# Filter halves written straight into their slots, the other half by one copy each, and `vlo` at the head of its iteration

## The chip, the cores and the metric

One core of a Trainium2 chip runs the kernel. The metric is the device time of one execution in microseconds; lower is better. Five engines work side by side, each with its own queue: TensorE (PE; its weight loads are shown as PEld), VectorE (DVE), ScalarE (ACT), GpSimd (POOL) and SyncE (SP), which issues nearly all DMAs.

## The reference, cut to what matters

Four blocks, each adding to `x` (64 samples, 64 channels, 1024 columns, fp32) the output of four modulated convolutions:

```python
def _layer(x, style, w, b, mw, mb, typ):
    s = style @ mw.T + mb
    weight = SCALE * w * s[:, None, :, None]
    weight = weight * lax.rsqrt(jnp.sum(weight * weight, axis=(2, 3)) + EPS)[:, :, None, None]
    if typ == 'same':         out = vmap(_conv_same)(x, weight) + b[None, :, None]
    elif typ == 'upsample':   out = _blur(vmap(_conv_up)(x, ...) + b[None, :, None], 2.0 * blur_k, (1, 1))
    elif typ == 'downsample': out = vmap(_conv_down)(_blur(x, blur_k, (2, 2)), weight) + b[None, :, None]
    return out
# TYPES = ('same', 'upsample', 'same', 'downsample'), kernel size 3, SCALE = 1/24, blur 1 3 3 1
for k in range(4):
    x = x + layers_of_block_k(x, cond_512)
```

## The kernel before, in words

A sample lies in SBUF as 128 rows: 64 channels of the odd columns and 64 of the even ones, 512 columns each. Layer 1 is one convolution (`conv0`, six matmuls of 512 columns). Layers 2 to 4 with both blurs are merged, for each sample, into one filter of seven taps (`g`), and `convg` applies it in twelve matmuls of 512 columns. Every operand is split into a high part in fp32r and the rest (`xh`/`xl`, `zh`/`zl`, `gh`/`gl` and so on), and three products are added: high by high, low by high, high by low. ScalarE writes the high parts, VectorE the low ones.

The loop runs over n = 0 to 255 (sample and block). In its iteration n TensorE runs `conv0(n+1)`, then `convg(n)`. ScalarE runs `xhi(n+3)` and `zhi(n+1)`; VectorE `xlo(n+3)`, `xnew(n-1)` (adds the result to `X`) and `zlo(n+1)`. The filters are made once for a quad of four samples, on an order written out by hand:

- GpSimd scales the weights (`w3s`) and takes their low part (`w3lo`); ScalarE takes the high part (`w3hi`, L731).
- TensorE's `v_products` follow `convg` in iterations n = 1 mod 4. In the next iteration VectorE's `vfull` (L1001) evicts them to `vf`, and ScalarE's `vhi` (L737) writes `vh` in two instructions, L741 and L742.
- `vlo` (L1010) on VectorE has three instructions: `v4` (L1013), `vl` (L1015) and the last part of `vh` (L1017). It stands behind `zlo` in iterations n = 3 mod 4.
- TensorE's `k_products` stand at the head of iterations n = 0 mod 4 and need `vh` and `vl`. ScalarE evicts them to `kp` (`kev`, L752), in two parts around `zhi`; in the last block `xb` (L724), which adds a bias to `X`, follows at the end of each iteration.
- In the following iteration VectorE filters `kp` into `gf` (`fir_even`, `fir_odd`). One later ScalarE copies the two end taps to `gf` (L767) and rounds all of `gf` into `sh` (L769, in `ghi`), VectorE subtracts into `sl` (L1063, in `glo`).
- SP's `spread` (L332) copies from there to `gh` and `gl`. These hold three pairs of samples, each pair with two samples by eight slots of 64 columns. In the upper 64 rows the seven taps lie in slots 0 to 6, in the lower 64 rows in slots 1 to 7; the slot left over is zero. The filters of a quad's first pair are made in the upper rows of `gf`, those of the second pair in the lower rows, and either has to be in both halves: four DMAs for `gh` and four for `gl`, of 224 KB. Before a pair is overwritten SP waits for `convg` of the pair three back. `convg` of a quad's first sample waits for all four `gh` DMAs (`ghd`) before its first matmul, and for the four of `gl` (`gld`) before its ninth.

Table work for the next block (`setup`) and the edge columns (`edge`) are put behind the ordinary work in certain iterations, most of them n = 3 mod 4.

Of the kernel before, what the change touches and what calls it, by code (L numbers as in the profile page):

```python
# [7 lines left out]
F32 = mybir.dt.float32  # L8
# [46 lines left out]
NT = 7  # L55
BLUR_E, BLUR_O, BLUR_M, BLUR_SUM = 6.0, 15.0, 20.0, 32.0
KS = 10
EVEN, ODD, CORR, NONE = slice(1, 8, 2), slice(2, 8, 2), 0, 9
# [29 lines left out]
def build(nc, x, ends, pack, taps, w3in, small, sets, out):  # L88
    ctx = ExitStack()
    with ctx:  # L90
        def sb(name, shape, dt=F32):
            return ctx.enter_context(nc.sbuf_tensor(name, shape, dt))
# [44 lines left out]
        sh = sb("sh", [128, 2, NT, C], F32R)  # L137
        sl = sb("sl", [128, 2, NT, C], F32R)
# [95 lines left out]
        def by_tap(a):  # L234
            return a.rearrange("p i t c -> p t i c")

        def landed(q):

            return 16 * (2 + 4 * q)
# [62 lines left out]
        def _(sp):  # L302
# [29 lines left out]
            def spread(q):  # L332

                first, second = 2 * q, 2 * q + 1
                for name, ready, of, to in (("ghd", "gsh", sh, gh), ("gld", "gsl", sl, gl)):
                    sp.wait_ge(s[ready], q + 1)
                    for h, rows in ((first, slice(0, C)), (second, slice(C, 128))):
                        if q == 0 and h == first:
                            continue
                        if h >= 3:  # L340
                            sp.wait_ge(s["convg"], 2 * (h - 2))
                        src = of[rows, :, :, :].bitcast(F32)
                        sp.dma_start(to[0:C, h % 3, :, 0:NT, :].bitcast(F32), src).then_inc(s[name], 16)  # L343
                        sp.dma_start(to[C:128, h % 3, :, 1:NT + 1, :].bitcast(F32), src).then_inc(s[name], 16)  # L344
# [301 lines left out]
        def _(act):  # L646
# [115 lines left out]
            def ghi(q):  # L762

                act.wait_ge(s["fir"], q + 1)
                if q >= 1:
                    act.wait_ge(s["ghd"], landed(q - 1))
                act.activation(gf[:, 0:NT:NT - 1], kp[:, 1:8:6], ACT.Copy).then_inc(s["gfe"], 1)  # L767
                act.wait_ge(s["gfe"], q)
                act.activation(by_tap(sh[:, :, :, :]), gf[:, :, :, :], ACT.Copy).then_inc(s["gsh"], 1)  # L769
# [7 lines left out]
            def ghi_rest():  # L777

                act.wait_ge(s["fir"], 1)
                act.activation(by_tap(sh[C:128]), gf[C:128], ACT.Copy).then_inc(s["gsh"], 1)  # L780
# [60 lines left out]
            for n in range(2, NN):  # L841
                if n + 3 < NN:
                    xhi(n + 3)
# [13 lines left out]
                if v_at(n + 2) is not None:  # L857
                    w3hi(v_at(n + 2))
# [5 lines left out]
        def _(dve):  # L864
# [195 lines left out]
            def glo(q):  # L1060
                dve.wait_ge(s["gsh"], q + 1)
                dve.wait_ge(s["gld"], landed(q - 1))
                dve.tensor_tensor(by_tap(sl[:, :, :, :]), gf[:, :, :, :], by_tap(sh[:, :, :, :]).bitcast(F32), ALU.subtract).then_inc(s["gsl"], 1)  # L1063
# [7 lines left out]
            def glo_rest():  # L1071
                dve.wait_ge(s["gsh"], 1)
                dve.tensor_tensor(by_tap(sl[C:128]), gf[C:128], by_tap(sh[C:128]).bitcast(F32), ALU.subtract).then_inc(s["gsl"], 1)
# [106 lines left out]
            for n in range(2, NN):  # L1180
                due = g_at(n - 1)
                if due is None and n + 3 < NN:
                    xlo(n + 3)
                xnew(n - 1)
                if due is not None:
                    dve.wait_ge(s["kev"], due + 1)
                    dve.wait_ge(s["gsh"], due)
                    fir_even(whole, both)
# [12 lines left out]
                if v_at(n - 2) is not None and n - 2 not in V_LATE:  # L1201
                    vlo(v_at(n - 2))
# [310 lines left out]
```

## Time and profile before

| | us |
|---|---|
| median of 3 runs (1399.49 to 1403.38) | 1401.16 |
| the profiled execution | 1402.98 |
| its span, first to last instruction | 1401.2 |
| TensorE busy in the span | 1325.6 |
| VectorE busy | 1101.9 |
| ScalarE busy | 784.6 |
| GpSimd busy | 327.1 |

The profile is of one execution. Busy time is the union of an engine's instructions; the end of a matmul is modelled, so a weight load (PEld) shows a stall more fully than a matmul does. "Idle before" is the time in which an engine had nothing to run ahead of an instruction, with the instruction or DMA that ended it.

### The profile page before, as it was taken

The numbers are of one execution on the slowest core, as the hardware profiler recorded it, in microseconds if no ns is written. First come the engines' busy times: TensorE is split into PE (matmuls) and PEld (weight loads), VectorE is DVE, ScalarE is ACT, GpSimd is POOL, SyncE is SP. The second block draws the span as 40 slices with busy tenths as digits, with TensorE's granted clock in tenths as the row PEclk, the third lists the DMA queues.
The fourth block names the chain that finished last, engine by engine and source line by source line (L and its number), as shares of the span: only waits on it lengthen the run. The fifth ranks groups of instructions, "written<-read, shape, count | busy, mean of one in ns | idle before, by whom it ended". The sixth has DMA issues, their size and how long they took to land.

```text
span 1401.2 us, 20330 instructions
## 1 busy us (share of the span) xinstructions
PE 1325.6 (95%) x6565; PEld 1085.8 (77%) x6565; DVE 1101.9 (79%) x1792; ACT 784.6 (56%) x1465; POOL 327.1 (23%) x632
## 2 busy tenths in 40 slices
PE   7799999999999999999999999999999999999998
PEld 5587877787888788788788777788787777777776
DVE  6788788887787878888787788888787667778764
ACT  5556465655555555555555555555556466665663
POOL 2213211132213212114122211213212232222210
PEclk9899999999999999999999999999999989999999
DMA  8457867677876658877766867677865497687664
GB/s 298 117 122 195 210 177 193 167 186 204 219 188 174 168 162 219 211 183 199 168 190 185 218 175 197 148 187 205 225 184 155 106 182 192 175 220 189 180 165 114
DMA packets 148201, 257.51 MB, mean 184 GB/s; under 512 B 14784, under 2 KB 81344, under 8 KB 148096
## 3 DMA queue, kind: packets, MB, share of 16 engines
q1 hardware_dynamic: 147728, 255.93, 70.9%
q8 instruction: 54, 0.88, 0.3%
q14 instruction: 51, 0.42, 0.1%
q10 hardware_dynamic: 368, 0.28, 0.1%
HBM read 72.39 MB, written 67.24 MB: 100 GB/s over the span
## 4 chain that ended last, share of the span: by engine, by line
PE 41%; DVE 23%; ACT 10%; issue 9%; DMA 7%; SPq 7%; POOL 2%; ACTq 0%; DVEq 0%; POOLq 0%
PE ps L463 40%; DMA gl<-sl 7%; DVE zl L978 4%; SPq L343 4%; ACT kp L750 4%; SPq L344 3%; DVE gf L1029 3%; DVE xl L972 3%; DVE X L987 3%; ACT xh L709 2%; DVE vl L1015 2%; DVE v L1013 2%; DVE vf L1008 1%; DVE vh L1017 1%; DVE gf L1035 1%
## 5 line engine op out<-in xcount | busy, mean ns | idle before, releaser
L463 PE MATMUL ps<-zh,gh 128*128 128x512 f32 (+1 forms) x1028 | 410.8, 400 | 9.9 <-DMA gh<-sh 4.5
L463 PE MATMUL ps<-zl,gh 128*128 128x512 f32 (+1 forms) x1028 | 407.7, 397 | 0.0
L721 ACT ACTIVATE zh<-ps,t_bx 128x512 fp32r<-128x512 f32 x256 | 176.2, 688 | 315.0 <-PE ps L463 312.8
L463 PE MATMUL ps<-zh,gl 128*128 128x512 f32 (+1 forms) x1028 | 285.0, 398 | 17.5 <-DMA gl<-sl 17.2
L750 ACT ACTIVATE kp<-ps,t_T1s 64x256 f32<-64x256 f32 x512 | 213.0, 464 | 157.6 <-PE ps L463 154.4
L987 DVE SCALAR_TENSOR_TENSOR X<-ps,t_D,X 128x512 f32<-128x512 f32 x255 | 190.2, 746 | 94.8 <-PE ps L463 73.7
L978 DVE SCALAR_TENSOR_TENSOR zl<-ps,t_bx,zh 128x512 fp32r<-128x512 f32 x256 | 191.1, 746 | 88.7 <-ACT zh L721 85.1
L972 DVE SCALAR_TENSOR_TENSOR xl<-X,t_S,xh 128x513 fp32r<-128x513 f32 x256 | 190.8, 765 | 78.5 <-ACT xh L709 77.2
L463 PEld LDWEIGHTS ps<-zh,gl 128*128 128x128 f32 x1028 | 191.2, 189 | 71.7 <-DMA gl<-sl 29.5
L463 PEld LDWEIGHTS ps<-zh,gh 128*128 128x128 f32 x1028 | 196.3, 191 | 60.6 <-issue 8.0
L463 PEld LDWEIGHTS ps<-zl,gh 128*128 128x128 f32 x1028 | 196.0, 191 | 45.2
L709 ACT ACTIVATE xh<-X,t_S 128x513 fp32r<-128x513 f32 x256 | 183.2, 716 | 1.2
L1280 POOL TENSOR_TENSOR w3h<-w3q,w3h 64x256 fp32r<-64x256 f32 x63 | 47.3, 751 | 581.5 <-ACT w3h L735 579.4
L463 PE MATMUL ps<-xh,w0l 128*128 128x512 f32 x512 | 164.5, 403 | 2.7 <-POOL w0l L1264 2.7
L463 PE MATMUL ps<-xh,w0h 128*128 128x512 f32 x512 | 163.0, 400 | 1.4 <-ACT xh L709 1.4
L463 PE MATMUL ps<-xl,w0h 128*128 128x512 f32 x512 | 163.0, 400 | 0.2 <-DVE xl L972 0.2
L1029 DVE SCALAR_TENSOR_TENSOR gf<-kp,gf 128x384 f32<-128x384 f32 (+1 forms) x260 | 145.6, 560 | 6.8
L463 PEld LDWEIGHTS ps<-xh,w0l 128*128 128x128 f32 x512 | 98.1, 192 | 26.7 <-POOL w0l L1264 3.1
L463 PEld LDWEIGHTS ps<-xl,w0h 128*128 128x128 f32 x512 | 98.1, 192 | 24.7 <-DVE xl L972 0.7
L463 PEld LDWEIGHTS ps<-xh,w0h 128*128 128x128 f32 x512 | 88.0, 190 | 12.9 <-ACT xh L709 1.6
L1274 POOL TENSOR_TENSOR w3q<-w3f,t_E 128x512 f32<-128x512 f32 x63 | 68.7, 1091 | 29.0 <-DVE xl L972 21.3
L463 PE MATMUL ps<-vl,w1h 128*128 128x256 f32 x256 | 46.3, 304 | 27.3 <-DVE vl L1015 27.3
(204 smaller groups left out, 1583.0 us busy)
## 6 DMA issues: line engine op xcount, KB each, us to landing
out_x<-X SPq DMA_DIRECT2D x255, 256.5 KB, 6.6
gh<-sh SPq DMA_DIRECT2D x254, 224.0 KB, 3.9
gl<-sl SPq DMA_DIRECT2D x254, 224.0 KB, 4.4
X<-out_x SPq DMA_DIRECT2D x96, 513.0 KB, 8.3
X<-x_in SPq DMA_DIRECT2D x32, 513.0 KB, 9.1
pk<-taps_in SPq DMA_DIRECT2D x3, 512.0 KB, 11.9
pk<-pack_in SPq DMA_DIRECT2D x3, 352.0 KB, 11.2
pk<-sets_in SPq DMA_DIRECT2D x4, 256.0 KB, 9.0
```

The costliest lines, as they stand in the source:

```text
L343: sp.dma_start(to[0:C, h % 3, :, 0:NT, :].bitcast(F32), src).then_inc(s[name], 16)
L344: sp.dma_start(to[C:128, h % 3, :, 1:NT + 1, :].bitcast(F32), src).then_inc(s[name], 16)
L463: return pe.matmul(out_ap, a, b, start=first, stop=last, skip_group_check=True)
L709: act.activation(xh[n % 3][:, 0:XW], X[:, sl, :], ACT.Copy, scale=tab["S0"][:, k, b:b + 1]) \
L721: act.activation(zh[n % 2][:, ZPAD:ZPAD + M], ps[:, ZP + n % 2, :], IDENT, bias=tab["bx"][:, k, b:b + 1]).then_inc(s["zhi"], 1)
L750: return act.activation(kp[rows, to, i, :], got[of, :, j, :], ACT.Copy, scale=tab["T1s"][of, k, b:b + 1])
L972: dve.scalar_tensor_tensor(xl[n % 3][:, 0:XW], X[:, sl, :], tab["S0"][:, k, b:b + 1], xh[n % 3][:, 0:XW].bitcast(F32), ALU.mult, ALU.subtr ...
L978: dve.scalar_tensor_tensor(zl[n % 2][:, ZPAD:ZPAD + M], ps[:, ZP + n % 2, :], tab["bx"][:, k, b:b + 1], zh[n % 2][:, ZPAD:ZPAD + M].bitcas ...
L987: dve.scalar_tensor_tensor(X[:, sl, 0:M], ps[:, OP + n % 2, :], tab["D3"][:, k, b:b + 1], X[:, sl, 0:M], ALU.mult, ALU.add).then_inc(s["xn ...
L1029: return dve.scalar_tensor_tensor(dve_out, kp[rows, of, i, :], factor, dve_out, ALU.mult, ALU.add)
L1274: sig(pool.tensor_tensor(w3q[:, :, :, :], w, e, ALU.mult), "w3q")
L1280: link(pool.tensor_tensor(w3h[C:128, 1], w3q[C:128, 1], hi[C:128, 1], ALU.subtract))
```

## The change

Filter halves. `sh` and `sl` are gone. `ghi` writes each pair of samples with its own ACTIVATE from its 64 rows of `gf` into those same rows of `gh`, and `glo` does so with its own subtraction into `gl`; both engines wait for `convg` themselves, and the waits for earlier DMAs are gone. `spread` copies, for each pair and part, only the other 64 rows, in one DMA of 960 contiguous fp32 a row (240 KB), the same columns shifted by one slot of 64. That makes four DMAs a quad, each issued as soon as its half is written.

Order. On VectorE `vlo` moves from behind `zlo` (and behind `vfull` and `glo`, where they stand) to the head of its iteration, before `xlo`. On ScalarE `w3hi` moves from the end of an iteration to the head of the next, which in the last block is behind `xb`.

```diff
@@ -55,6 +55,7 @@
 NT = 7
 BLUR_E, BLUR_O, BLUR_M, BLUR_SUM = 6.0, 15.0, 20.0, 32.0
 KS = 10
+PAIR = 2 * (NT + 1) * C
 EVEN, ODD, CORR, NONE = slice(1, 8, 2), slice(2, 8, 2), 0, 9
 ZP, OP, VG, EP = 0, 2, 4, 6
 LEFT, RIGHT = 0, 1
@@ -134,8 +135,6 @@
         v4 = sb("v4", [128, QS, C])
         kp = sb("kp", [128, KS, 2, C])
         gf = sb("gf", [128, NT, 2, C])
-        sh = sb("sh", [128, 2, NT, C], F32R)
-        sl = sb("sl", [128, 2, NT, C], F32R)
         gh = sb("gh", [128, 3, 2, NT + 1, C], F32R)
         gl = sb("gl", [128, 3, 2, NT + 1, C], F32R)
 
@@ -231,12 +230,16 @@
             q, i = divmod(n + G_LEAD, QS)
             return q if i == 0 and 0 <= q < NQ else None
 
-        def by_tap(a):
-            return a.rearrange("p i t c -> p t i c")
+        def flat(a):
+            return a.rearrange("p i t c -> p (i t c)")
+
+        def own(a, h):
+            rows, slots = ((slice(0, C), slice(0, NT)), (slice(C, 128), slice(1, NT + 1)))[h % 2]
+            return rows, a[rows, h % 3, :, slots, :].rearrange("p i t c -> p t i c")
 
         def landed(q):
 
-            return 16 * (2 + 4 * q)
+            return 16 * (1 + 2 * q)
 
         def edge_at(n):
 
@@ -331,17 +334,14 @@
 
             def spread(q):
 
-                first, second = 2 * q, 2 * q + 1
-                for name, ready, of, to in (("ghd", "gsh", sh, gh), ("gld", "gsl", sl, gl)):
-                    sp.wait_ge(s[ready], q + 1)
-                    for h, rows in ((first, slice(0, C)), (second, slice(C, 128))):
-                        if q == 0 and h == first:
-                            continue
-                        if h >= 3:
-                            sp.wait_ge(s["convg"], 2 * (h - 2))
-                        src = of[rows, :, :, :].bitcast(F32)
-                        sp.dma_start(to[0:C, h % 3, :, 0:NT, :].bitcast(F32), src).then_inc(s[name], 16)
-                        sp.dma_start(to[C:128, h % 3, :, 1:NT + 1, :].bitcast(F32), src).then_inc(s[name], 16)
+                for name, ready, of in (("ghd", "gsh", gh), ("gld", "gsl", gl)):
+                    for h in ((2 * q, 2 * q + 1) if q else (1,)):
+                        sp.wait_ge(s[ready], h)
+                        a = flat(of[:, h % 3]).bitcast(F32)
+                        if h % 2 == 0:
+                            sp.dma_start(a[C:128, C:], a[0:C, 0:PAIR - C]).then_inc(s[name], 16)
+                        else:
+                            sp.dma_start(a[0:C, 0:PAIR - C], a[C:128, C:]).then_inc(s[name], 16)
 
             sp.dma_start(misc[:, 0:HEAD], small[:, 0:HEAD]).then_inc(s["c_small"], 16)
             sp.dma_start(misc[:, HEAD:SMALL], small[:, HEAD:SMALL]).then_inc(s["coef"], 16)
@@ -762,11 +762,12 @@
             def ghi(q):
 
                 act.wait_ge(s["fir"], q + 1)
-                if q >= 1:
-                    act.wait_ge(s["ghd"], landed(q - 1))
                 act.activation(gf[:, 0:NT:NT - 1], kp[:, 1:8:6], ACT.Copy).then_inc(s["gfe"], 1)
                 act.wait_ge(s["gfe"], q)
-                act.activation(by_tap(sh[:, :, :, :]), gf[:, :, :, :], ACT.Copy).then_inc(s["gsh"], 1)
+                for h in (2 * q, 2 * q + 1):
+                    act.wait_ge(s["convg"], 2 * max(h - 2, 0))
+                    rows, dst = own(gh, h)
+                    act.activation(dst, gf[rows], ACT.Copy).then_inc(s["gsh"], 1)
 
             def ghi_first(i):
 
@@ -777,7 +778,8 @@
             def ghi_rest():
 
                 act.wait_ge(s["fir"], 1)
-                act.activation(by_tap(sh[C:128]), gf[C:128], ACT.Copy).then_inc(s["gsh"], 1)
+                rows, dst = own(gh, 1)
+                act.activation(dst, gf[rows], ACT.Copy).then_inc(s["gsh"], 1)
 
             act.wait_ge(s["warm"], 1)
             act.activation(warm[:, :], warm[:, :], ACT.Sqrt)
@@ -839,6 +841,8 @@
             kev(1, 1)
             w3hi(2)
             for n in range(2, NN):
+                if v_at(n + 1) is not None and n + 1 not in V_LATE:
+                    w3hi(v_at(n + 1))
                 if n + 3 < NN:
                     xhi(n + 3)
                 if g_at(n) is not None:
@@ -854,8 +858,6 @@
                 k, stages = setup_at(n)
                 for stage in stages:
                     setup(k, stage)
-                if v_at(n + 2) is not None:
-                    w3hi(v_at(n + 2))
                 if where(n)[1] == NBLK - 1:
                     xb(n)
 
@@ -1058,9 +1060,11 @@
             whole, both = slice(0, 128), slice(0, 2)
 
             def glo(q):
-                dve.wait_ge(s["gsh"], q + 1)
-                dve.wait_ge(s["gld"], landed(q - 1))
-                dve.tensor_tensor(by_tap(sl[:, :, :, :]), gf[:, :, :, :], by_tap(sh[:, :, :, :]).bitcast(F32), ALU.subtract).then_inc(s["gsl"], 1)
+                for h in (2 * q, 2 * q + 1):
+                    dve.wait_ge(s["gsh"], h)
+                    dve.wait_ge(s["convg"], 2 * max(h - 2, 0))
+                    rows, dst = own(gl, h)
+                    dve.tensor_tensor(dst, gf[rows], own(gh, h)[1].bitcast(F32), ALU.subtract).then_inc(s["gsl"], 1)
 
             def glo_first(i):
                 dve.wait_ge(s[("gh0", "gh1")[i]], 1)
@@ -1070,7 +1074,8 @@
 
             def glo_rest():
                 dve.wait_ge(s["gsh"], 1)
-                dve.tensor_tensor(by_tap(sl[C:128]), gf[C:128], by_tap(sh[C:128]).bitcast(F32), ALU.subtract).then_inc(s["gsl"], 1)
+                rows, dst = own(gl, 1)
+                dve.tensor_tensor(dst, gf[rows], own(gh, 1)[1].bitcast(F32), ALU.subtract).then_inc(s["gsl"], 1)
 
             def edge(k, stage):
 
@@ -1179,12 +1184,14 @@
             xlo(4)
             for n in range(2, NN):
                 due = g_at(n - 1)
+                if v_at(n - 2) is not None and n - 2 not in V_LATE:
+                    vlo(v_at(n - 2))
                 if due is None and n + 3 < NN:
                     xlo(n + 3)
                 xnew(n - 1)
                 if due is not None:
                     dve.wait_ge(s["kev"], due + 1)
-                    dve.wait_ge(s["gsh"], due)
+                    dve.wait_ge(s["gsh"], 2 * due - 1)
                     fir_even(whole, both)
                 if n + 1 < NN:
                     zlo(n + 1)
@@ -1198,8 +1205,6 @@
                     glo(g_at(n - 2))
                 if n - 1 in V_LATE:
                     vlo(v_at(n - 1))
-                if v_at(n - 2) is not None and n - 2 not in V_LATE:
-                    vlo(v_at(n - 2))
                 if edge_at(n)[0] is not None:
                     edge(*edge_at(n))
                     for job in behind(*edge_at(n)):
```

## Rows read from the trace of the kernel before

**Rows 1.** The page: busy us (share of the span) xinstructions; one group of loads (mean ns | idle before).

```profile
PE 1325.6 (95%) x6565; PEld 1085.8 (77%) x6565; DVE 1101.9 (79%) x1792; ACT 784.6 (56%) x1465; POOL 327.1 (23%) x632
...
L463 PEld LDWEIGHTS ps<-zl,gh 128*128 128x128 f32 x1028 | 196.0, 191 | 45.2
```

**Rows 2.** Waits of the weight loads, whole run: us in total, times, longest us.

```profile
PEld ps L463 <- DVE vl L1015: 32.2, 24, 3.5
PEld ps L463 <- DMA gl<-sl: 29.5, 32, 2.3
...
PEld ps L463 <- DVE vh L1017: 11.0, 18, 1.2
PEld ps L463 <- DVE zl L978: 6.6, 11, 1.4
```

**Rows 3.** Timeline of the weight loads, third and last block: start us, us, ... [idle before <-releaser].

```profile
1011.47 0.19 PEld L463 LDWEIGHTS ps<-zh,gh 128*128 128x128 f32 x1
...
1014.30 0.76 PEld L463 LDWEIGHTS ps<-zh,gl 128*128 128x128 f32 x4 [1.00 <-DMA gl<-sl]
...
1031.08 0.19 PEld L463 LDWEIGHTS ps<-vh,w1d 128*128 128x128 f32 x1 [0.64 <-DVE vh L1017]
...
1034.68 0.78 PEld L463 LDWEIGHTS ps<-zh,gl 128*128 128x128 f32 x4 [0.15 <-DMA gl<-sl]
...
1209.71 0.54 PEld L463 LDWEIGHTS ps<-vl,w1h 128*128 128x128 f32 x4 [1.70 <-DVE vl L1015]
...
1231.06 0.54 PEld L463 LDWEIGHTS ps<-vl,w1h 128*128 128x128 f32 x4 [1.66 <-DVE vl L1015]
```

**Rows 4.** Timeline of VectorE, one quad of the third block.

```profile
1003.91 1.08 DVE L1063 TENSOR_TENSOR sl<-gf,sh 128x896 fp32r<-128x896 f32 x1
1005.62 0.76 DVE L972 SCALAR_TENSOR_TENSOR xl<-X,t_S,xh 128x513 fp32r<-128x513 f32 x1 [0.63 <-ACT xh L709]
...
1006.95 0.74 DVE L978 SCALAR_TENSOR_TENSOR zl<-ps,t_bx,zh 128x512 fp32r<-128x512 f32 x1
1007.72 0.43 DVE L1013 TENSOR_TENSOR v<-vf,vh 64x256 f32<-64x256 f32 x1
1008.18 1.12 DVE L1015 TENSOR_TENSOR vl<-vf,vh 128x512 fp32r<-128x512 f32 x1
1009.33 0.42 DVE L1017 TENSOR_TENSOR vh<-v,vf 64x256 fp32r<-64x256 f32 x1
```

**Rows 5.** Groups by line and form, whole run: busy us, mean ns | idle before us <-releasers.

```profile
L1063 DVE TENSOR_TENSOR sl<-gf,sh 128x896 fp32r<-128x896 f32 x63 | 70.5, 1119 | 0.0
...
L769 ACT ACTIVATE sh<-gf 128x896 fp32r<-128x896 f32 x63 | 60.1, 953 | 2.0
...
L767 ACT ACTIVATE gf<-kp 128x256 f32<-128x256 f32 x63 | 25.7, 408 | 1.7 <-DVE gf L1029 1.7
L742 ACT ACTIVATE vh<-vf 64x256 fp32r<-64x256 f32 x64 | 25.7, 402 | 0.0
```

**Rows 6.** Timeline of ScalarE, the quad of rows 4.

```profile
1004.56 0.40 ACT L742 ACTIVATE vh<-vf 64x256 fp32r<-64x256 f32 x1
```

**Rows 7.** Timeline of SP's queue, the quad of rows 4, its last copy.

```profile
1009.65 0.94 SPq L344 DMA_DIRECT2D gl<-sl  x1
```

**Rows 8.** DMA issues, whole run: count, KB each, median us from issue to landing.

```profile
gl<-sl SPq DMA_DIRECT2D x254, 224.0 KB, 4.4
```

**Rows 9.** Timelines of ScalarE, VectorE and GpSimd, last block.

```profile
1210.85 1.67 ACT L750 ACTIVATE kp<-ps,t_T1s 64x256 f32<-64x256 f32 x4 [3.15 <-PE ps L463]
...
1215.78 0.75 DVE L987 SCALAR_TENSOR_TENSOR X<-ps,t_D,X 128x512 f32<-128x512 f32 x1 [1.77 <-ACT X L729]
...
1224.45 1.31 DVE L1063 TENSOR_TENSOR sl<-gf,sh 128x896 fp32r<-128x896 f32 x1
...
1207.52 1.01 DVE L1013 TENSOR_TENSOR v<-vf,vh 64x256 f32<-64x256 f32 x1
...
1207.51 0.74 POOL L1280 TENSOR_TENSOR w3h<-w3q,w3h 64x256 fp32r<-64x256 f32 x1
```

## The prediction

> **What bounds the kernel now.** I read the page's busy shares first: TensorE is busy 95% of the span [rows 1], so whatever it waits for sets the end. Because a matmul's end is modelled, I then took the waits of the weight loads, where a stall shows whole [rows 2]. Three waits stand out, and all three belong to the once-a-quad filter work: 32.2 us for `vl` (24 times), 29.5 us for the DMA that brings `gl` (32 times), 11.0 us for `vh` (18 times). The fourth, `zl`, is 6.6 us. The timeline of the weight loads [rows 3] says what a quad (four samples) costs without them: from 1014.30 to 1034.68 are 20.38 us, of which 0.64 and 0.15 are such stalls, so 19.59; in the last block 21.35 us, of which 1.66 are a stall, so 19.69. I take 19.6 us. The stalls are therefore whole losses, and nothing else hides behind them.
>
> Why they exist is in VectorE's timeline [rows 4]. Behind `glo` (1003.91, 1.08 us) VectorE waits 0.63 us for `xh`, runs `xlo`, `xnew` and `zlo`, and only then begins the three operations of `vlo` (1007.72), which end at 1009.75. This quad just makes it; the next is 0.64 us late for `vh`, and in the last block each is 1.7 us late for `vl` [rows 3]. The `gl` chain is long for another reason: `glo` ends at 1004.99, but SP still has `gh` copies to issue, and the last of the eight copies is issued at 1009.65 [rows 7] and lands some 4.4 us later [rows 8], after TensorE wanted it at 1013.30 (1014.30 less 1.00).
>
> **The change part by part.** (1) *`vlo` goes to the head of its iteration.* Its inputs are ready then: `vh`'s second part ends at 1004.96 [rows 6]. This takes `vlo` out of the queue behind `zlo`, whose own input comes late. Gain: up to 32.2 + 11.0 us less the ordinary gap of 0.044 us between loads (45.2 us over 1028 in the page's group of loads that wait for nothing [rows 1]) for each of 42 events: 41.4 us.
>
> (2) *Half the copies.* SP issues four DMAs of 240 KB a quad instead of eight of 224 KB, and sends each as soon as its half is written. In the quad of [rows 4] the second half of `glo` would end at 1004.99 + 1.08 = 1006.07; its copy, issued at about 1006.1, lands near 1010.5 by the 4.4 us of [rows 8], 2.8 us before the 1013.30 at which it is wanted. The longest `gl` wait was 2.3 us, at a landing that is now some 3.5 us earlier, so all of the 29.5 us go, less 32 x 0.044: 28.1 us. The `gh` copies leave earlier than the `gl` ones and were not waited for in steady state.
>
> (3) *What it adds.* `sh` and `sl` were written once with all 128 rows; `gh` and `gl` are written in two instructions of 64 rows, each with the same 896 columns. ScalarE's 64-row and 128-row copies of 256 columns take 402 and 408 ns [rows 5], so half the rows save nothing. Each quad gets one more ACTIVATE of 953 ns and one more subtraction of 1119 ns [rows 5], 60 and 70 us of busy time in 63 quads. Is it covered? On ScalarE it pushes `vhi` back: `vh`'s second part would end at about 1004.96 + 0.95 = 1005.91, before VectorE is free at 1006.07, so nothing is late. On VectorE: `vlo` from 1006.1 for 2.03 us (1007.72 to 1009.75), then `xlo`, `xnew`, `zlo` for 2.07 us (1005.62 to 1007.69), done at 1010.2; `vl` is ready at 1007.7 instead of 1009.3. The products that need this `zlo` start at 1011.47 [rows 3]. So 1.2 us are to spare, and that cover is thin: any further 1.2 us of VectorE work in that stretch is paid by TensorE. The 70 us cost nothing in plain quads. They do cost in quads with table work or an edge stage, which put 1 to 3 us more on VectorE in the third iteration. Bounds: nothing at all below; above, the whole added 1.12 us in each of about 10 such quads in each of three blocks and 4 in the last, 38 us. Most of that work runs just before the one iteration of the four in which VectorE has only its three ordinary operations, so I take about a quarter, 8 us. Today's `zl` waits, 6.6 us in 11 places [rows 2], say that these places are few.
>
> (4) *The waits that move.* ScalarE and VectorE now wait for `convg` themselves before they overwrite a third buffer. Both instructions stand behind `zhi`/`zlo` of a later sample, whose products TensorE runs after the `convg` in question, so the wait is already met: 0. The old waits for `ghd` and `gld` go, also 0. SP's queue gets shorter; a store behind the copies leaves earlier, and no engine waits for a store here.
>
> (5) *`w3hi`.* End of one iteration to start of the next: the same place in three blocks; in the last it comes behind `xb`, 0.7 us later, with over an iteration to spare. 0.
>
> **The last block has to be looked at alone**, since there the quad is not TensorE's but a ring: K products, ScalarE's `kev` and `xb` (1210.85 until VectorE starts at 1215.78: 4.93 us), VectorE until `glo` (1224.45: 8.67 us), `glo`, `xlo` to `zlo`, `vlo`, K products again [rows 9]. The new ring is 4.93 + 8.67 + 1.31 + 1.08 (two halves) + 0.46 + 1.13 (to the end of `vl`) + 1.14 (seven products, 1209.71 to 1210.85) = 18.7 us. That is under 19.6, so TensorE sets the pace there too, with 0.9 us left. Here VectorE and GpSimd collide: the 64-row subtraction `v` takes 1.01 us when it starts with GpSimd's L1280 at 1207.5 [rows 9] and 0.43 us in the quad of [rows 4], 0.58 us more. With one more such hold the ring is 19.3. I put 4 us on the last block for quads where two holds meet.
>
> The Trainium skill speaks against the change at this point (SBUF — State Buffer, section "SBUF: two separate sides"): a VectorE instruction with two SBUF inputs and a GpSimd instruction lock each other out for a whole instruction. The trace agrees in the 1.01 against 0.43 us above. By that rule each new subtraction is one more candidate to be held, and the time would go towards the first rival's 1377 us instead of my sum.
>
> **Sum.** -41.4 - 28.1 + 8 + 4 = -57.5 us on the profiled span of 1401.2 us: 1343.7 us. The profiled execution took 1402.98 us (1.8 around its span), 1.8 above the median of 1401.16; taken from the median, 1343.7 us. The lower bound: nothing is added, and the 6.6 us of `zl` waits, less the ordinary gap in 11 of them, go as well: 1401.2 - 69.5 - 6.1 = 1325.6.
>
> **The rivals.** *VectorE is held in every quad.* If each quad loses its slack to GpSimd and 0.55 us more, 61 quads cost 34 us: 1377 us. For it: VectorE is at 1101.9 us today [rows 1] and goes to some 1172 in a shorter span, and the held 1.31 us `glo` [rows 9]. Against it: the `glo` of [rows 4] took 1.08 us, unheld, and the mean over 63 is 1.12 [rows 5].
>
> *The landing, not the chain, is what is late.* If a copy queued behind loads and stores lands when it did, whatever its issue, the 28.1 us of `gl` stay: 1371.8 us. For it: 4.4 us from issue to landing [rows 8] is long for one copy, so others stand before it. Against it: those others are mostly these same copies, and their bytes nearly halve.
>
> *It doesn't do what it says.* `gl` and `vl` come earlier, but TensorE waits as long for the next thing, `zl`: 57.5 us over 61 quads are 0.94 us each, on top of the 1.2 us of slack; within 0.3% of 1401. That needs the walk to be 2.1 us short in every quad.
>
> *Slower.* The place is `zlo` behind `vlo`: `zl` is now what TensorE meets last. Its price is everything beyond 1.2 us of slack, times 61. It becomes a loss when the walk is short by over 2.2 us a quad, for instance if both halves cost twice their row and the ScalarE half holds VectorE: at 2.6 us, 1343.7 + 61 x 1.4 = 1429 us. Nothing in the rows shows a 64-row instruction dearer than a full one, but none of this shape is there.
>
> **Chances.** My sum 0.66 (its own range 1325 to 1362), VectorE held 0.14, landing 0.08, no difference 0.04, slower 0.08. Faster by over 0.3% (about what a measurement can tell from no change, 4 us) is the first three, 0.88; same 0.04; slower 0.08. The range takes in the first three with their bounds: 1325 to 1382. Predicted 1343 us.
>
> **What the changed profile would show.** Right: no weight load waits for `vl`, `vh` or `gl` beyond a few; `gh<-gh` and `gl<-gl` copies, 127 each; two 64x896 instructions a quad on ScalarE (near 0.95 us) and VectorE (near 1.08 us); quads of 19.6 us in all blocks. Wrong: `zl` at the head of the waits, 64x896 subtractions at 1.3 us or more, or `gl` waits that stay. If quads come at 19.6 us and the total misses, it is the table and edge quads of part 3.

## The result and the profile after

The changed kernel takes **1336.21 us** (median of 4 runs, 1335.82 to 1336.43) against 1401.01 us for the kernel before in the same comparison (4 runs, 1399.49 to 1403.38). The ratio is **0.9536, 95% interval 0.9519 to 0.9552**: 64.8 us faster. The forecast was 1343 us, with its own range 1325 to 1362.

The busy line of the page after, next to the line of before in [rows 1]:

```profile
PE 1301.2 (98%) x6565; PEld 1077.7 (81%) x6565; DVE 1150.0 (86%) x1855; ACT 842.1 (63%) x1528; POOL 347.3 (26%) x632
```

The number of matmuls is the same; TensorE's share went from 95% to 98% of a span that is now 1334.3 us. VectorE has 63 instructions more, as said, but only 48.1 us more of busy time, not 70. What TensorE's loads wait for, whole run (us in total, times, longest us), against [rows 2]:

```profile
PEld ps L463 <- DVE zl L980: 20.7, 24, 2.6
PEld ps L463 <- issue: 9.8, 5, 4.1
...
PEld ps L463 <- DVE vl L1017: 1.7, 2, 1.3
...
PEld ps L463 <- DVE vh L1019: 0.6, 2, 0.3
```

The 43.2 us of `vl` and `vh` have become 2.3, the 29.5 us of `gl` have vanished from the list, and `zl` has grown from 6.6 to 20.7 us. Together 79.3 us became 23.0. A quad without table or edge work now has no stall at all. The timeline of the loads that open each quad's K products, second block:

```profile
591.17 0.54 PEld L463 LDWEIGHTS ps<-vl,w1h 128*128 128x128 f32 x4
...
610.76 0.54 PEld L463 LDWEIGHTS ps<-vl,w1h 128*128 128x128 f32 x4
```

19.59 us apart, with no idle time in brackets (the quad before is 19.60): the 19.6 us that the prediction read out of [rows 3]. The copies (count, KB each, median us from issue to landing) against [rows 8]:

```profile
gh<-gh SPq DMA_DIRECT2D x127, 240.0 KB, 3.0
gl<-gl SPq DMA_DIRECT2D x127, 240.0 KB, 3.6
```

The `gl` copies land in 3.6 us where they took 4.4. The page's line for the DMA queue is `q1 hardware_dynamic: 94896, 201.81, 52.7%` (packets, MB, share); before it was 147728 packets, 255.93 MB, 70.9%.

The timelines of VectorE, SP's queue and TensorE's loads in one plain quad are the counterpart of [rows 3, 4, 7]:

```profile
605.41 2.19 DVE L1067 TENSOR_TENSOR gl<-gf,gh 64x896 fp32r<-64x896 f32 x2
607.64 0.42 DVE L1015 TENSOR_TENSOR v<-vf,vh 64x256 f32<-64x256 f32 x1
608.09 0.69 DVE L1017 TENSOR_TENSOR vl<-vf,vh 128x512 fp32r<-128x512 f32 x1
608.81 0.42 DVE L1019 TENSOR_TENSOR vh<-v,vf 64x256 fp32r<-64x256 f32 x1
609.27 1.12 DVE L974 SCALAR_TENSOR_TENSOR xl<-X,t_S,xh 128x513 fp32r<-128x513 f32 x1
...
610.97 0.74 DVE L980 SCALAR_TENSOR_TENSOR zl<-ps,t_bx,zh 128x512 fp32r<-128x512 f32 x1
```

```profile
607.63 0.46 SPq L344 DMA_DIRECT2D gl<-gl  x1
```

```profile
612.87 0.19 PEld L463 LDWEIGHTS ps<-zh,gh 128*128 128x128 f32 x1
```

`glo` ends at 607.60 and its last copy is issued 0.03 us later, where SP was 4.66 us behind before. `zlo` ends at 611.71 and TensorE wants it at 612.87: 1.16 us to spare, against the 1.2 us of part 3. And `vlo`'s middle instruction takes 0.69 us where it took 1.12 in [rows 4]. The reason is in GpSimd's timeline:

```profile
608.87 0.97 POOL L1285 TENSOR_TENSOR w3h<-w3q,w3h 64x256 fp32r<-64x256 f32 x1 [16.28 <-ACT w3h L735]
```

`w3lo` now starts when the first two instructions of `vlo` are over. It falls on `xlo` instead (1.12 us) and on `xnew` and `zlo`, which it doesn't stretch (0.74 us for `zlo`, as in [rows 4]). Groups of VectorE's instructions by form (busy us, mean ns | idle before), whole run, after and then before:

```profile
L974 DVE SCALAR_TENSOR_TENSOR xl<-X,t_S,xh 128x513 fp32r<-128x513 f32 x256 | 202.1, 809 | 35.0 <-ACT xh L709 32.8
L1067 DVE TENSOR_TENSOR gl<-gf,gh 64x896 fp32r<-64x896 f32 x126 | 138.6, 1100 | 2.0
...
L1017 DVE TENSOR_TENSOR vl<-vf,vh 128x512 fp32r<-128x512 f32 x64 | 45.4, 710 | 2.0
L1019 DVE TENSOR_TENSOR vh<-v,vf 64x256 fp32r<-64x256 f32 x64 | 32.9, 514 | 2.0
L1015 DVE TENSOR_TENSOR v<-vf,vh 64x256 f32<-64x256 f32 x64 | 26.9, 420 | 2.7 <-ACT vh L742 0.8
```

```profile
L972 DVE SCALAR_TENSOR_TENSOR xl<-X,t_S,xh 128x513 fp32r<-128x513 f32 x256 | 190.8, 765 | 78.5 <-ACT xh L709 77.2
L1015 DVE TENSOR_TENSOR vl<-vf,vh 128x512 fp32r<-128x512 f32 x64 | 62.8, 982 | 2.0
L1017 DVE TENSOR_TENSOR vh<-v,vf 64x256 fp32r<-64x256 f32 x64 | 41.4, 646 | 2.0
L1013 DVE TENSOR_TENSOR v<-vf,vh 64x256 f32<-64x256 f32 x64 | 34.9, 546 | 2.7 <-ACT vh L742 0.8
```

`glo` costs 68.1 us more (138.6 less the 70.5 of [rows 5]), `vlo` 33.9 us less in its three instructions, `xlo` 11.3 more: 45.5 of the 48.1.

### The profile page after: what moved, and what is told of

The parts are those of the page before. It is cut to its first block, busy times and chain, and to the rows that moved or that the text cites. A ratio compares the mean times of both kernels' runs of the same rounds, so it can differ in the third digit from the quotient of the medians.

```text
span 1334.3 us, 20141 instructions
## 1 busy us (share of the span) xinstructions
PE 1301.2 (98%) x6565; PEld 1077.7 (81%) x6565; DVE 1150.0 (86%) x1855; ACT 842.1 (63%) x1528; POOL 347.3 (26%) x632
## 3 DMA queue, kind: packets, MB, share of 16 engines
q1 hardware_dynamic: 94896, 201.81, 52.7%
## 4 chain that ended last, share of the span: by engine, by line
PE 75%; DVE 15%; ACT 4%; issue 3%; POOL 2%; DMA 1%; SPq 0%; ACTq 0%; DVEq 0%; POOLq 0%
PE ps L463 74%; ACT kp L750 2%; DVE gl L1067 2%; DVE gf L1031 2%; DVE zl L980 2%; DVE xl L974 2%; DVE X L989 1%; DVE vf L1010 1%; DVE gf L1037 1%; ACT xh L709 1%; DVE vl L1017 1%; DVE vh L1019 1%; POOL w3q L1279 1%; DVE v L1015 0%; DVE gf L1043 0%
## 5 line engine op out<-in xcount | busy, mean ns | idle before, releaser
L463 PEld LDWEIGHTS ps<-zh,gh 128*128 128x128 f32 x1028 | 195.0, 190 | 70.0 <-DVE zl L980 20.7
L974 DVE SCALAR_TENSOR_TENSOR xl<-X,t_S,xh 128x513 fp32r<-128x513 f32 x256 | 202.1, 809 | 35.0 <-ACT xh L709 32.8
L980 DVE SCALAR_TENSOR_TENSOR zl<-ps,t_bx,zh 128x512 fp32r<-128x512 f32 x256 | 190.7, 745 | 48.1 <-ACT zh L721 45.2
L463 PEld LDWEIGHTS ps<-zh,gl 128*128 128x128 f32 x1028 | 194.7, 189 | 45.4
L1285 POOL TENSOR_TENSOR w3h<-w3q,w3h 64x256 fp32r<-64x256 f32 x63 | 59.6, 946 | 537.5 <-ACT w3h L735 535.5
L463 PE MATMUL ps<-xh,w0l 128*128 128x512 f32 x512 | 161.7, 397 | 2.7 <-POOL w0l L1269 2.7
L1031 DVE SCALAR_TENSOR_TENSOR gf<-kp,gf 128x384 f32<-128x384 f32 (+1 forms) x260 | 148.6, 572 | 6.8
L1067 DVE TENSOR_TENSOR gl<-gf,gh 64x896 fp32r<-64x896 f32 x126 | 138.6, 1100 | 2.0
L770 ACT ACTIVATE gh<-gf 64x896 fp32r<-64x896 f32 x126 | 120.2, 954 | 3.6
```

Source lines behind the costliest of these rows:

```text
L463: return pe.matmul(out_ap, a, b, start=first, stop=last, skip_group_check=True)
L770: act.activation(dst, gf[rows], ACT.Copy).then_inc(s["gsh"], 1)
L974: dve.scalar_tensor_tensor(xl[n % 3][:, 0:XW], X[:, sl, :], tab["S0"][:, k, b:b + 1], xh[n % 3][:, 0:XW].bitcast(F32), ALU.mult, ALU.subtr ...
L980: dve.scalar_tensor_tensor(zl[n % 2][:, ZPAD:ZPAD + M], ps[:, ZP + n % 2, :], tab["bx"][:, k, b:b + 1], zh[n % 2][:, ZPAD:ZPAD + M].bitcas ...
L1031: return dve.scalar_tensor_tensor(dve_out, kp[rows, of, i, :], factor, dve_out, ALU.mult, ALU.add)
L1067: dve.tensor_tensor(dst, gf[rows], own(gh, h)[1].bitcast(F32), ALU.subtract).then_inc(s["gsl"], 1)
```

## The experiments

The theory was that each part of the change takes away one of two late things, that neither is worth much alone, and that what remains afterwards is 1.2 us of slack on VectorE's way to `zlo`. The rivals were that one part does it all, that traffic or the number of DMAs is what made `gl` late, and, for the 20.7 us of `zl` that remain, VectorE's own table work against ScalarE being held in its queue. The times of the kernel before differ a little between the three sets of runs (medians 1401.52, 1404.8 and 1407.0 us); the ratios allow for that, and within a set the times compare directly. The changed kernel was not in the first set (e1 to e4), so there it is compared by the ratio.

**The order alone** (e1): the kernel before with `vlo` and `w3hi` moved, and nothing else; the part for `vlo`:

```diff
+                if v_at(n - 2) is not None and n - 2 not in V_LATE:
+                    vlo(v_at(n - 2))
                 if due is None and n + 3 < NN:
                     xlo(n + 3)
...
-                if v_at(n - 2) is not None and n - 2 not in V_LATE:
-                    vlo(v_at(n - 2))
```

> The kernel before with the order alone changed (vlo at the head of its iteration, w3hi at the head of the next), sh, sl and the eight copies kept. My theory (two chains that end close together): the vl and vh waits go, but TensorE then comes earlier to the products with gl, whose last copy still lands when it did; the gl waits grow to some 45 to 60 us, and the time is 1375 to 1390 us, a good deal less than the 41 us that the vl and vh waits measured. Rival (the parts add up): the gl waits stay at 29.5 us and the time is near 1360 us.

Measured: 1384.1 us, ratio 0.9867 (0.9836 to 0.9897). Its waits:

```profile
PEld ps L463 <- DMA gl<-sl: 59.9, 57, 2.7
...
PEld ps L463 <- DVE zl L978: 2.4, 6, 0.7
```

`vl` and `vh` are gone from the list, but of their 43.2 us 30.4 came back as waits for `gl`, in 57 places instead of 32. TensorE simply met the copy earlier. So 17 us of gain, not 41, as expected.

**The halves alone** (e2): the changed kernel with both moves undone.

> The changed kernel with the order of before (vlo behind zlo, w3hi at the end of its iteration), the halves written straight into their slots and four copies a quad kept. My theory: the gl waits go (28 us), but the added ACTIVATE holds xh and so xlo and vlo back by about 0.95 us, and plain quads in which vl was just in time now wait that long: 61 x 0.95 = 58 us more. Time about 1430 us, slower than before. Rival (the parts add up): 1401 - 28 + 8 = 1381 us.

Measured: 1410.99 us, ratio 1.0071 (1.0043 to 1.0099): slower. No `gl` wait is left, and:

```profile
PEld ps L463 <- DVE vl L1017: 70.0, 58, 3.7
...
PEld ps L463 <- DVE vh L1019: 5.7, 9, 1.2
```

The expected mechanism came, but not its size: 1430 us was expected and 1381 if the parts add up, and the time lies between them. The `gl` waits go (29.5 us), those of `vl` and `vh` grow by 32.5 us (43.2 to 75.7) where 58 were expected, and `zl` by 4.2 (6.6 to 10.8). The second subtraction and the second ACTIVATE stand ahead of `vlo` and push it back in nearly every quad (58 waits instead of 24); which of the two does more was not separated. Halving the copies by itself gives nothing that TensorE can use. The two parts alone multiply to 0.9867 x 1.0071 = 0.9937; together they are 0.9536. Some 4%, 56 us of the 65, exist only in the combination.

**One subtraction more** (e3) and **two more** (e4): ahead of `glo`, `gf` less `gh` is also written to a tile that nobody reads, for one half or for both.

```diff
                 for h in (2 * q, 2 * q + 1):
...
+                    if h % 2 == 0:
+                        dve.wait_ge(s["ext"], q - 1)
+                        dve.tensor_tensor(extra[rows], gf[rows], own(gh, h)[1].bitcast(F32), ALU.subtract).then_inc(s["ext"], 1)
```

> The changed kernel with one more 64x896 subtraction a quad on VectorE, ahead of glo's first half, into a tile that nobody reads (1.1 us a quad, 69 us of busy time in all). My theory: in plain quads zl is ready 1.16 us before it is wanted in three blocks and 0.8 us in the last, so the extra work is nearly covered: 0.3 us in each of 13 quads, and up to 1.1 us in some 10 to 15 edge quads, 5 to 15 us in all, 1341 to 1351 us. Rival 1 (VectorE is the bound): 61 x 1.1 = 67 us, 1403 us. Rival 2 (VectorE has room everywhere, it is busy only 86%): no change, 1336 us.

> As the run with one extra subtraction, but two of them a quad (2.2 us). My theory: beyond the slack everything is paid: 2.2 - 1.16 in 48 quads and 2.2 - 0.8 in 13, 68 us, and a little in the edge quads; about 1405 to 1415 us. The step from one extra to two is 60 us or more though the first cost 5 to 15. Rival 1 (VectorE is the bound): equal steps of 67 us, 1470 us. Rival 2: no change.

Measured: 1387.22 us (1385.98 to 1388.0, ratio 0.9892) and 1459.17 us (1458.32 to 1461.62, ratio 1.0409). The expectations for both were missed: 1387 where 1341 to 1351 stood, 1459 where 1405 to 1415 stood. The rival of equal steps (67 and 67 us) doesn't fit either: the steps are 50 and 72 us. By my account 1.1 us more should have just fitted into 1.16 us of slack, and it cost about 50 us, 0.8 us a quad as a mean. The waits with one more:

```profile
PEld ps L464 <- DVE zl L981: 51.8, 61, 2.7
PEld ps L464 <- DVE vl L1018: 15.5, 15, 2.8
```

The timeline of VectorE in one of its most stretched quads, and that of GpSimd:

```profile
616.37 1.11 DVE L1018 TENSOR_TENSOR vl<-vf,vh 128x512 fp32r<-128x512 f32 x1
617.51 0.85 DVE L1020 TENSOR_TENSOR vh<-v,vf 64x256 fp32r<-64x256 f32 x1
618.39 1.44 DVE L975 SCALAR_TENSOR_TENSOR xl<-X,t_S,xh 128x513 fp32r<-128x513 f32 x1
```

```profile
615.93 1.00 POOL L1289 TENSOR_TENSOR w3h<-w3q,w3h 64x256 fp32r<-64x256 f32 x1 [11.11 <-ACT w3h L736]
617.01 1.06 POOL L1290 TENSOR_TENSOR w3l<-w3q,w3h 128x256 fp32r<-128x256 f32 x1
```

GpSimd's `w3lo` (and `w3q` at 618.25 behind it) keeps its place and `vlo` has moved onto it: 1.11, 0.85 and 1.44 us where the changed kernel has 0.69, 0.42 and 1.12. In this quad the extra 1.08 us thus became 2.25 us, and the slack was 1.16. (This is the rule cited in the prediction, the Trainium skill, SBUF — State Buffer, section "SBUF: two separate sides". The rows agree: GpSimd's subtraction ends at 616.93, and with VectorE's own 0.69 us behind it that would be 617.62, against a measured end of 617.48, so VectorE lost nearly all of the rest of that instruction.)

Not every quad is like this one. From the first instruction of `glo` (or the extra one) to the end of `zlo`, VectorE's path grew by 1.0 to 1.1 us in 28 of the 59 quads from the fifth to the last but one, by 1.4 to 1.9 us in 19 and by 2.2 to 2.6 us in 12, 1.4 us as a mean; the whole run agrees, with 88.2 us more of VectorE's busy time, 69.8 of it the extra subtraction itself. The time from one of these quads to the next grew by 47.7 us in all. 4.6 us of that stand in 12 quads of the last block and 13.7 in 13 edge quads at the starts of blocks, about what the expectation had (5 to 15 us). The other 29 us stand in 34 quads of the first three blocks, most of which were expected to cost nothing, and there `vlo` or `xlo` is stretched by GpSimd. The expectation for two more had the second step right (60 us or more) and fell with the first. The second extra subtraction costs 72 us, 1.14 us a quad, its whole duration: by then there is little slack to hide anything.

**The copies twice** (e8): each of the four copies is preceded by the same copy into a tile that nobody reads. **Small ones beside them** (e10): the same, with the additional copies cut to 64 columns, 16 KB.

```diff
+                        if h % 2 == 0:
+                            sp.dma_start(junk[C:128, j], a[0:C, 0:PAIR - C]).then_inc(s["jk"], 16)
+                        else:
+                            sp.dma_start(junk[0:C, j], a[C:128, C:]).then_inc(s["jk"], 16)
```

> The changed kernel with every copy issued twice, first into a tile that nobody reads, so that count and bytes are those of before while the halves are still written directly. My theory (it is the chain up to the last issue that was late, not the traffic): gl has some 2.8 us to spare, each second issue takes about 0.5 us and the landing about 1 us more, so no waits come back beyond a few; 1336 to 1342 us. Rival (the traffic made the landing late): the gl waits come back, 1336 + 28 = 1364 us.

> Each of the four copies a quad is preceded by a small one of 16 KB from the same rows into a tile that nobody reads: eight issues a quad as in the kernel before, bytes nearly as in the changed one. If the number of issues makes the copies late, SP still needs 1 us for each as with the doubled copies, gl waits of some 60 to 90 us come back and the time is 1390 to 1430 us. If the bytes do, SP's issues stay near 0.46 us, the last gl copy is issued at most 1 us later than in the changed kernel and lands in time: 1336 to 1345 us with gl waits under 5 us.

Measured: 1427.57 us (ratio 1.016, 1.0133 to 1.0187) against 1339.09 us (ratio 0.9516, 0.9492 to 0.9541; the changed kernel had 0.9503, 0.9479 to 0.9526, beside it). Both have eight issues a quad. The DMA table and the waits with full copies, and then SP's queue in one quad:

```profile
gl<-gl SPq DMA_DIRECT2D x127, 240.0 KB, 5.3
```

```profile
PEld ps L471 <- DMA gl<-gl: 92.9, 62, 4.0
```

```profile
622.56 1.04 SPq L349 DMA_DIRECT2D gl<-gl  x1
...
624.27 1.02 SPq L351 DMA_DIRECT2D gl<-gl  x1
```

The same with small ones:

```profile
gl<-gl SPq DMA_DIRECT2D x127, 240.0 KB, 3.3
```

```profile
PEld ps L471 <- DMA gl<-gl: 0.2, 1, 0.2
```

```profile
609.17 0.60 SPq L351 DMA_DIRECT2D gl<-gl  x1
```

With the bytes of the kernel before (264 MB against 256) the waits for `gl` come back and exceed its 29.5 us. The fairer yardstick is e1, where no late `vl` hides them: 59.9 us. In e8 each copy also stands directly behind its twin of the same size, which the kernel before didn't have. With its number of issues but few bytes (206 MB) the waits don't come back. The last `gl` copy of the small variant is issued 1.9 us after `glo` ends and still arrives in time; that of the full one 3.3 us after, and such a copy takes 5.3 us instead of 3.3 to land (medians of the runs). The bytes lengthen both, the landing and SP's own issues (1.02 to 1.04 us in these rows against 0.60; 0.94 in [rows 7]). The expectation for e8, that its copies would still land in time, fell; the rival named there was right in kind and too small. e10 came out as the bytes have it in its time and its `gl` waits, though its issues took 0.54 to 0.60 us in this quad instead of some 0.46, and the last was issued 1.9 us behind `glo` where at most 1 us more than in the changed kernel (0.03) was expected.

**`w3hi` behind `kev`, in all iterations** (e6), and **the root an iteration later as well** (e7). These go after the `zl` waits that remain. ScalarE's timeline of the changed kernel in one of these places, and the load that is late at the end of it:

```profile
756.78 0.63 ACT L735 ACTIVATE w3h<-w3q 128x512 fp32r<-128x512 f32 x1 [6.07 <-POOL w3q L1279]
```

```profile
761.14 0.19 PEld L463 LDWEIGHTS ps<-zh,gh 128*128 128x128 f32 x1 [1.22 <-DVE zl L980]
```

ScalarE waits 6.07 us for GpSimd's `w3q`; `xhi`, `kev` and `zhi` stand behind it, and `zhi` starts only at 759.62. Over the run `w3h` waits so for 59.0 us in 10 places. GpSimd's timeline has the reason:

```profile
755.32 0.32 POOL L1388 TENSOR_TENSOR en<-en,t_c 64x64 f32<-64x64 f32 x1 [7.23 <-DVE en L1106]
755.71 1.04 POOL L1279 TENSOR_TENSOR w3q<-w3f,t_E 128x512 f32<-128x512 f32 x1
```

It is itself held for 7.23 us, by an edge stage of VectorE (`en`, L1106), with the scaling of the weights behind its own edge stage. So the wait runs through the queues of three engines.

> The changed kernel with w3hi moved on behind kev's second part in the same iteration. In the changed kernel the waits for zl (20.7 us in 24 places) stand in quads with edge work, and there ScalarE is held by w3hi, which waits up to 6 us for GpSimd's w3q, so that zhi and then zlo are late. My theory: behind kev, w3hi holds nobody; about half of the zl waits go, 8 to 12 us less than the changed kernel, 1325 to 1328 us. Rival (my step of the prediction: it is VectorE's own table and edge work that makes zl late): no change.

> As the run with w3hi late, and the square root of the table work moved on ScalarE by one iteration too; today it waits for VectorE's reciprocal in front of xhi and kev (5.4 us once a block, zl 1.7 us late behind it). My theory: another 1.7 us in each of three blocks, 5 us, so 1320 to 1323 us. Rival: as above, no change.

Measured: 1347.88 us (1346.85 to 1349.25, ratio 0.9585) and 1342.27 us (1339.16 to 1343.24, ratio 0.9539), against 1339.16 us (1337.81 to 1340.41, ratio 0.9523) for the changed kernel in the same set. Both expectations were missed, and for e6 "no change" was wrong as well. The 1.22 us wait above is gone in e6, and the one at the root in e7, which gains 5.6 us on e6 where 5 were expected; yet e6 is 8.7 us slower than the changed kernel. Its waits:

```profile
PEld ps L463 <- DVE zl L980: 30.8, 44, 2.5
PEld ps L463 <- DVE vl L1017: 8.3, 18, 1.2
```

VectorE is busy 1206.0 us instead of 1150. Moving `w3hi` moves GpSimd's `w3lo` behind it, now onto the filter, as VectorE's timeline of e6 shows beside GpSimd's:

```profile
602.58 0.80 DVE L1035 TENSOR_TENSOR kp<-kp 128x128 f32<-128x128 f32 x1
603.42 1.18 DVE L1037 SCALAR_TENSOR_TENSOR gf<-kp 128x512 f32<-128x512 f32 x1
604.53 1.13 DVE L1039 SCALAR_TENSOR_TENSOR gf<-kp 128x128 f32<-128x128 f32 x1
```

```profile
602.50 0.74 POOL L1285 TENSOR_TENSOR w3h<-w3q,w3h 64x256 fp32r<-64x256 f32 x1 [14.21 <-ACT w3h L735]
...
604.23 1.28 POOL L1279 TENSOR_TENSOR w3q<-w3f,t_E 128x512 f32<-128x512 f32 x1 [0.17 <-POOL w3l L1286]
```

Unheld, these three take 0.28, 0.69 and 0.28 us. Over the run the filter's five largest groups, these three among them, take 78 us more than in the changed kernel. The head of the iteration is therefore not a free choice: in plain quads it puts `w3lo` beside `xlo`, `xnew` and `zlo`, and the last two, which read PSUM, aren't stretched by it. The filter reads and writes SBUF alone.

**`w3hi` late only where it is held** (e9): in two iterations a block, and the root an iteration later.

```diff
+            def late(n):
+                return n in (20, 24) or n >= NB and n % NB in (8, 12)
...
-                if v_at(n + 1) is not None and n + 1 not in V_LATE:
+                if v_at(n + 1) is not None and n + 1 not in V_LATE and not late(n):
                     w3hi(v_at(n + 1))
...
                 if g_at(n) is not None:
                     kev(g_at(n), 1)
+                if v_at(n + 1) is not None and n + 1 not in V_LATE and late(n):
+                    w3hi(v_at(n + 1))
...
-                    setup(k, stage)
+                    if stage != RECIP:
+                        setup(k, stage)
+                k, stages = setup_at(n - 1)
+                if RECIP in stages:
+                    setup(k, RECIP)
```

> w3hi behind kev only in those iterations where ScalarE stood behind GpSimd's w3q (two a block), and the root a iteration later; all else as the changed kernel. If the remaining zl waits come from ScalarE held in order, the waits of 1.2 to 1.8 us in the edge and setup quads go, some 9 to 12 us of the 20.7, and VectorE's busy time stays at 1150 us: 1326 to 1331 us. Rival (VectorE's own table and edge work is what is late, as the prediction's part 3 has it): the waits stay and the time is that of the changed kernel, 1336 to 1340 us.

> The changed kernel once more, as the yardstick of this call: 1336 to 1340 us, ratio to the kernel before 0.952 to 0.956.

Measured: **1323.59 us (1322.64 to 1324.18), ratio 0.9405 (0.9382 to 0.9429)**, against 1337.13 us (1336.84 to 1337.76), ratio 0.9503 (0.9479 to 0.9526), for the changed kernel in the same set: 13.5 us faster than it, a little better than expected (1326 to 1331), and the best version found. The changed kernel's time came as expected, its ratio just under the 0.952 to 0.956. Its waits:

```profile
PEld ps L463 <- issue: 12.0, 6, 4.7
PEld ps L463 <- DVE zl L989: 5.9, 11, 0.9
```

`zl` goes from 20.4 us (23 times, in the changed kernel of this set) to 5.9, 14.5 us less, which is the whole 14.0 us between the two spans (1336.0 and 1322.0). `w3h` now waits for `w3q` 5.1 us in 2 places instead of 59.0 in 10. ScalarE's timeline of the quad above has it without a wait, and no load waits for `zl` between 745 and 769 us:

```profile
752.46 0.63 ACT L735 ACTIVATE w3h<-w3q 128x512 fp32r<-128x512 f32 x1
```

**`w3hi` back at its old place** (e5), everything else as changed.

> Only the move of w3hi is undone (end of the iteration before, in place of the head of the next). The prediction prices this at nothing: within 2 us of the changed kernel, 1335 to 1341 us. Rival: w3hi's place sets when GpSimd's w3lo runs, and with it a collision in the last block: 3 to 8 us slower.

Measured: 1339.56 us (1338.75 to 1341.67, ratio 0.9521), 2.4 us more than the changed kernel beside it (1336.84 to 1337.76): small, but the ranges don't overlap. It is within the range expected and just over the 2 us allowed for. `zl` is 22.7 us in 26 places; the 2.3 us more stand at the start of the last block (longest wait 3.3 us instead of 2.7), which is the place that the rival named, for a little less than its 3 to 8 us.

**The changed kernel again** was run beside e6 and e7.

> The changed kernel once more, as the measure for the other three runs beside it: 1336 us, 0.9536 of before.

Measured: 1339.16 us, ratio 0.9523 (0.9499 to 0.9546).

## Why the prediction was right, point by point

The sum was -57.5 us; the measured difference is -64.8, and 66.9 between the profiled spans (1401.2 and 1334.3).

1. *`vlo` early, -41.4.* `vl` and `vh` fell by 40.9 us. Right as a term of this sum, but not as a price of this edit: alone it is worth 17 us (e1).
2. *Half the copies, -28.1.* All of the `gl` waits went. Here too the term holds only beside the other: alone the halves cost 10 us (e2). The prediction had the earlier issue as the whole cause, and it was more than that: bytes matter through the issues and the landing alike, as e8 brings the waits back by bytes, and e10 shows that eight issues with few bytes don't. How the gain divides between the earlier issue and the lighter traffic was not measured. The landing of 3.6 us was not foreseen; I had kept 4.4.
3. *What it adds, +8, and the last block, +4.* `zl` rose by 14.1 us against these 12. The size is nearly right, the place is not: I put it on VectorE's table and edge work as load. It is in such quads, but by way of GpSimd and ScalarE, which wait for an edge stage in order: e9 removes 14.5 us by moving ScalarE's `w3hi` and root behind the work that they held, with VectorE's instructions unchanged (1159.5 us busy, even more than 1150.1). In e1, without the second subtraction, `zl` is 2.4 us although ScalarE is held there too (`w3h` waits 53.2 us in 11 places); there TensorE is also late for `gl`, which helps `zl`. That the thinner slack is needed beside the hold is therefore argued and not shown; that taking the hold away is enough is shown. The ring in the last block was forecast at 18.7 us. In the changed trace ScalarE begins a K eviction at 1200.01, `vl` ends at 1216.55 + 0.69 = 1217.24, and 17.23 us and the 1.14 of the seven products are 18.4 us, under the 19.6 as said.
4. *Slack 1.2 us, quads of 19.6 us.* Measured 1.16 and 19.6. "Any further 1.2 us of VectorE work in that stretch is paid": in fact 1.1 us was enough, since a shift of `vlo` also puts it onto GpSimd's instructions in many quads (e3).
5. *The moved waits, 0.* No row after shows one of them.
6. *`w3hi`, 0.* Off by 2.4 us in this place (e5). The order is far more sensitive the other way: 8.7 us when `w3hi` comes behind `kev` in the same iteration (e6).
7. *The 1.12 us more a quad, 70 us busy.* VectorE grew by only 48, since `vlo` escaped `w3lo`: by the groups above 0.13 + 0.27 + 0.13 = 0.53 us a quad less. The prediction priced `vlo` at its old, held 2.03 us; that the slack still came out as forecast is because `xlo` was held in its place (1.12 us against 0.76 in [rows 4]).

Luck has a part in how near the sum came: +8 was right in size for a cause that was not the one named, and `vlo`'s shorter and `xlo`'s longer time cancel (point 7). The upper ends of the two ranges, 1362 and 1382, come out of no sum in the prediction; its own upper bound of 38 us in part 3 would give 1374.

The term that the sum lacks is a second-order one. By the spans, the waits of `vl`, `vh`, `gl` and `zl` give -56.3, or -53.8 less the ordinary gap of 57 events, 3.7 short of the sum; "issue" waits fell from 13.0 to 9.8 us, -3.2. The mean granted clock rose from 0.987 to 0.991, which is 5 us over the span. The lower level of the clock is seen in the kernel before at 1140 to 1150 us. TensorE is idle from 1140.0 until a load that had waited 3.53 us for `vl` starts at 1143.35. In windows of 1 us the granted clock is 1.00 until 1142 and 0.50, the 1.2 GHz level, from 1143 to 1149, with 3 to 6 matmuls in each; over the 10 us it is 0.66, with 21 matmuls. The same stretch of the kernel after has no such stall, a clock of 1.00 (2.4 GHz) and 51 matmuls. The 1.86 us wait for `vl` that ends at 1118.62 is followed by a low stretch too (0.50 at 1119 to 1122). The fall comes within or right behind the idle time in both; that the stall brought it about was not tested. Some 5 us of the 66.9 are left unassigned.

Of the rivals, *VectorE is held in every quad* did not occur: the new subtractions took 1.10 us as a mean. e3 shows how near it was, since 1.1 us more on VectorE brings a good part of it about. *The landing is late* is refuted by the vanished `gl` waits and came true in e8. *It doesn't do what it says* and *slower* needed the walk to be over 2 us short, and it has 1.16 us to spare; e4, at 1459 us, is how the second of them looks.

What stays open: why the `issue` waits (9.8 us, longest 4.1) are there, how much of the 5 us of clock comes from which stall, and which part of the `gl` gain is the earlier issue.

## What to carry to other kernels

When two chains are late by turns at the same engine, neither fix alone shows its worth: price the second wait as if the first were gone, and measure both together (here -17 and +10 us alone, -65 together). Before putting work onto an engine with measured slack, look at what the shift makes it collide with, not only at the slack: with 1.16 us of slack, 1.08 us of work became about 2.2 us in a fifth of the quads, and 29 of the 48 us it cost stand in quads where GpSimd stretched it. And in a queue that is served in order, an instruction with a late input is moved only where it is held: the same move gained 13 us in eight places (with the root in three more) and cost 9 us when made everywhere without it (3 us with it).

## What the runs showed of the hardware

- VectorE and GpSimd stretch each other, by nearly the whole rest of the instruction that started first. In the traces of the kernels before and after, e3 and e6, a VectorE instruction with its inputs in SBUF that starts over 0.25 us before the end of a GpSimd `w3h`, `w3l` or `w3q` ends 0.13 to 0.20 us earlier than GpSimd's end plus its own unheld duration, in 449 of 451 cases. So the 128x512 subtraction took 1.11 us instead of 0.69, the 64x256 one 0.85 instead of 0.42, and a 128x512 scalar_tensor_tensor 1.18 instead of 0.69. GpSimd's 64x256 subtraction took 0.74 us in most quads before, and 0.97 in the quad above, where VectorE's had started first.
- A VectorE instruction with one input in PSUM (`xnew`, `zlo`, `vfull`) isn't stretched beside the same GpSimd instructions: by 0.016 us at most in 133 cases of these four traces.
- A DMA of 240 KB between partitions landed in 3.1 to 3.6 us (medians of the `gl` copies) with 202 to 206 MB moved in the run, and in 5.3 us with 264 MB, each behind a twin of the same size (e8).
- Issuing a `gl` copy occupied SP for 0.46 us (median) in the kernel after, 0.60 in e10, 0.93 in the kernel before and 1.04 in e8. More traffic thus delays a copy twice, in SP's queue and on the way.
- Two 64-row subtractions of 896 columns took 1.10 us each, about as long as one of 128 rows (1.12): half the rows saved nothing.
